# Half-head tiles for RoPE, and values stored as rows of tokens, in a two-layer transformer kernel

## The chip, the cores and the metric

One core of one Trainium2 chip runs the whole program. A core has TensorE (matrix products into PSUM), VectorE, ScalarE, GpSimd and SyncE, which here only issues DMAs; 16 DMA engines move data between SBUF and HBM. The metric is device microseconds of one execution. Profiles come from one further execution.

## The reference

Input x is (2, 1024, 512) in float32. Four blocks follow, each added to x: attention A, a feed-forward block with LoRA, attention B, the same feed-forward block again. The change touches attention A, and of B only how values are stored. Attention A, with 32 heads of 16:

```python
q = (xn @ Wq).reshape(B, S, H, Dh)          # xn: layer norm of x
kv_latent = xn @ Wc                          # 64 wide
k = (kv_latent @ Wk).reshape(B, S, H, Dh)
v = (kv_latent @ Wv).reshape(B, S, H, Dh)
q = q * cos + rotate_half(q) * sin           # rotate_half: [-x2, x1] of a head's two halves
k = k * cos + rotate_half(k) * sin
probs = softmax(q @ k.T / sqrt(Dh))          # no mask
x = x + (probs @ v) @ Wo
```

Attention B has a causal mask, ALiBi and biases, and no RoPE.

## The kernel before, in words

The program runs in stages, with a meeting of all engines between two: `project_a` (projections of A), the run of attention A, `output_and_ffn` (which also projects B's queries, keys and values), the run of attention B, and a last `output_and_ffn`. Within a stage each engine has its own written order of work, and semaphores alone tie the engines.

`project_a` works on NC = 4 chunks of 512 tokens, two for each of the two sequences. TensorE's order in chunk c: the latent; query tile 0; the four key tiles (128 dimensions = 8 heads, by 512 tokens); the four value tiles (128 tokens by 512); the rotated key tiles; the turns (transposes) of the next chunk's normalised input; query tiles 1, 2, two rotated tiles, query tile 3, two rotated tiles. A rotated tile is a product of a constant +1/-1 matrix `rot` with the plain tile (L1050 to L1057). The tasks take the 8 PSUM banks in turn (`bank_plan`), in the last chunk five banks, since three then belong to the early maxima of the first attention's scores.

The path of one tile i (0 to 3 keys, 4 to 7 queries), number n = 8c + i: ScalarE copies the product to SBUF (`copy_plain`, L1111); GpSimd multiplies by the cosines (L1190, three buffers, so it runs at most three tiles ahead); VectorE multiplies the rotated tile, out of PSUM, by the sines (L1220) and adds (L1224), giving `roped`; ScalarE rounds it to the high part (`high`, L1124), VectorE takes the low part (`low`, L1229), one tile behind; SyncE stores both parts. There are four buffers of parts: `high` waits until the store of four tiles ago has landed.

Values: ScalarE copies a tile out of PSUM into one of two buffers (L1156); from the third tile on it waits for the landing of the store of two tiles ago.

ScalarE's order in a chunk: key copies 0 to 3; value tiles 0 to 3; high 0, 1, turned input; high 2, turned input, query copy 1; high 3, query copies 2, 3; high 4, 5; the next chunk's latent and query copy 0; high 6, 7. VectorE's: tiles 0 to 3 with the low parts behind them, the low parts of the turned input, tiles 4 and 5, the normalisation of chunk c + 2 (for c = 0 and 1), tiles 6, 7. In the last chunk VectorE also takes maxima of early score pieces (L358).

SyncE's order in chunk c: the four value stores of chunk c, then the stores of the 8 tiles. So the value stores of chunk c + 1 are issued after the last query store of chunk c. In chunk 2 it also issues the first loads for the attention, between the tile stores.

Stores of attention A and B alike: `store_parts` (L778 to L788) stores a key tile with one issue (both parts, 128 rows), a query tile with two issues (64 rows and both parts each, one for each group of 4 heads). The order of rows in HBM is head by head, 16 dimensions a head. A value tile goes with one issue (L999, L1494) in 8 pieces of 512 bytes per token, one per group, so that a group's load (`load_v`, L109) reads 4 KB rows.

After the meeting the run of attention A begins: SyncE and GpSimd wait until all stores have landed; GpSimd clears two slots (L116), issues key loads (L87) and splits the first maxima (L281); TensorE makes score pieces and turns those split maxima (L331) before the first scores (L607).

Of the kernel before, what the change touches and what calls it, by code (L numbers as in the profile page):

```python
# [55 lines left out]
class Slot:  # L56
# [735 lines left out]
def stored_counts(uses):  # L792

    return 16 * (uses + uses // 2)


class Stores:
# [3 lines left out]
    def __init__(self, nc, ctx, tag):  # L801
        self.parts = [ctx.enter_context(nc.semaphore(f"{tag}_parts_stored{i}")) for i in range(PARTS)]
        self.v = [ctx.enter_context(nc.semaphore(f"{tag}_v_stored{i}")) for i in range(2)]

    def wait(self, e, batches):
        for i in range(PARTS):
            e.wait_ge(self.parts[i], stored_counts(batches * 2 * 2 * KC // PARTS))
# [78 lines left out]
def project_a(nc, env, first, early):  # L886
# [6 lines left out]
    for c in range(NC):  # L893
# [18 lines left out]
    with ExitStack() as ctx:  # L912
# [11 lines left out]
        rot = sb("rot", [P, P])  # L924
# [28 lines left out]
        cos_ready = sem("cos_ready")  # L953
        roped_ready = sem("roped_ready")
# [7 lines left out]
        def _(sp):  # L962
            for name in ("ident", "minus_half"):
                sp.dma_start(consts[name][:, :], env["ins"][name]).then_inc(consts_loaded, 16)
            for c in range(NC):
# [3 lines left out]
                if c == 0:  # L969
# [12 lines left out]
                    for t, name in ((cos, "cos"), (sin, "sin"), (rot, "rot")):  # L982
# [9 lines left out]
            for c in range(NC):  # L992
                b, half = c // 2, c % 2

                def store_v():
                    for t in range(TPC):
# [3 lines left out]
                            env["va_d"].rearrange("(g p) (k c) -> p g k c", p=P, k=8)[  # L1000
                                :, b * GPB:(b + 1) * GPB, half * TPC + t, :],
                            vt[:, n % 2, :, :].rearrange("p (g h) c -> p g (h c)", h=GH)).then_inc(v_stored[n % 2], 16)
                store_v()
                for i in range(PT):
                    n = c * PT + i
                    sp.wait_ge(low_ready, n + 1)
                    store_parts(sp, env["qa_d"], env["ka_d"], c, i, parts[:, n % PARTS, :, :],
# [19 lines left out]
        def _(pe):  # L1027
# [21 lines left out]
            pe.wait_ge(table_loaded, 48)  # L1049
            for c in range(NC):  # L1050
                def rotated(i):
                    task = ("rotated", c, i)
                    banks.wait_empty(pe, task)

                    banks.wait_drained(pe, plain_task(c, i))
                    pe.matmul(banks.out(task), rot[:, :], plain(i),
                              start=True, stop=True).then_inc(banks.fill(task), 1)  # L1057
# [26 lines left out]
                for i in range(KC):  # L1084
# [803 lines left out]
```

## Time and profile before

| what | us |
|---|---|
| median of 3 runs | 1765.24 (1760.79 to 1771.05) |
| the profiled execution | 1764.37 |
| its span | 1762.2 |
| TensorE busy | 1643.6 (93%) |
| VectorE busy | 1402.5 (80%) |
| ScalarE busy | 969.0 (55%) |
| GpSimd busy | 213.8 (12%) |
| `project_a`, to the meeting | about 184 |

Times in rows are microseconds from the span's start unless they are called ns. PE is TensorE, PEld its weight loads, DVE VectorE, ACT ScalarE, POOL GpSimd, SPq SyncE's issues. L12 is line 12 of the kernel; a tensor is named by the memory that it lies in, so `w_q` is `roped` and the product with the sines, `w_o` the value buffers, `o_memory` and `w_proj` the plain tiles and the product with the cosines. In brackets stands the idle time before an instruction and what ended it.

### The profile page before, as it was taken

How to read it: one execution, taken by the hardware profiler on the slowest of the kernel's cores; microseconds unless marked ns; L12 is line 12 of the kernel's file. 1: busy time of each engine (PE TensorE's matmuls, PEld its weight loads, DVE VectorE, ACT ScalarE, POOL GpSimd, SP SyncE). 2: the span in 40 equal slices, each digit the busy share in tenths (PEclk: the TensorE clock that was granted, in tenths of full speed). 3: DMA queues.
4: the chain of work that ended last, by engine and by line, in shares of the span. 5: the costliest groups of instructions: out<-in, count | busy, mean ns of one | idle time of the engine just before them, and what ended most of it. 6: DMA issues, size and time to landing. Idle time of an engine off the chain costs nothing. (4 is left out here: it accounts for less than half of the span.)

```text
span 1762.2 us, 32974 instructions
## 1 busy us (share of the span) xinstructions
PE 1643.6 (93%) x13040; PEld 848.8 (48%) x13040; DVE 1402.5 (80%) x2959; ACT 969.0 (55%) x1095; POOL 213.8 (12%) x272
## 2 busy tenths in 40 slices
PE   6898999999999999999999999999999999999888
PEld 3554333333333333333344777655545555554667
DVE  3776799999999999999548364568898888899675
ACT  2433277777777777777821112126666666667210
POOL 3332200000000000000013021020101000003331
PEclk9999699999999999999999999989999999999999
DMA  7766433333333333331140433773645454542211
GB/s 212 224 169 197 91 57 61 75 62 61 61 60 62 62 61 65 61 59 59 57 157 24 143 102 112 213 158 58 112 82 92 77 93 78 95 77 87 88 69 72
DMA packets 116801, 167.58 MB, mean 95 GB/s; under 512 B 20772, under 2 KB 58036, under 8 KB 116532
## 3 DMA queue, kind: packets, MB, share of 16 engines
q1 hardware_dynamic: 115176, 160.99, 39.8%
q0 software_dynamic: 1472, 4.49, 1.3%
q8 instruction: 103, 1.69, 0.4%
q14 instruction: 50, 0.41, 0.1%
HBM read 100.41 MB, written 64.50 MB: 94 GB/s over the span
## 5 line engine op out<-in xcount | busy, mean ns | idle before, releaser
L358 DVE TENSOR_REDUCE mxp<-ps_m 128x1 f32<-128x512 f32 x1280 | 798.7, 684 | 69.5 <-PE ps_m L324 64.2
L686 ACT ACTIVATE a_p<-a_ps_s 128x1024 f32<-128x1024 f32 x512 | 522.6, 1025 | 149.1 <-PE a_ps_s L607 132.4
L686 ACT ACTIVATE b_p<-b_ps_s 128x1024 f32<-128x1024 f32 (+1 forms) x320 | 294.9, 939 | 158.5 <-PE b_ps_s L607 155.2
L355 DVE CUSTOM_DVE_ANT_0 ps_m<-ps_m,b_masks 128x128 f32<-128x128 f32 (+3 forms) x512 | 240.0, 517 | 43.6 <-PE ps_m L324 39.5
L324 PE MATMUL ps_m<-slot_qk 62*128 62x512 f32 (+3 forms) x624 | 230.9, 451 | 12.2 <-DVE mxp L358 8.9
L324 PE MATMUL ps_m<-a_slot_qk 62*128 62x512 f32 x640 | 237.6, 449 | 0.8
L607 PE MATMUL a_ps_s<-a_slot_qk 64*128 64x512 f32 x640 | 231.6, 442 | 1.7 <-DMA a_slot_qk<-cturned 0.5
L631 PE MATMUL a_ps_o<-a_p,a_slot_v 128*32 128x256 f32 x2560 | 205.6, 390 | 9.9 <-ACT a_p L686 5.4
L607 PEld LDWEIGHTS a_ps_s<-a_slot_qk 64*128 64x128 f32 x640 | 96.2, 185 | 129.4 <-issue 122.7
L281 POOL CAST cparts<-negm 128x16 fp32r<-128x16 f32 x64 | 12.6, 197 | 1119.3 <-DVE negm L364 1119.3
L607 PE MATMUL a_ps_s<-slot_qk 64*128 64x512 f32 x384 | 136.4, 455 | 0.7
L631 PE MATMUL a_ps_o<-a_p,slot_memory 128*32 128x256 f32 x1536 | 124.1, 393 | 7.3 <-ACT a_p L686 3.3
L324 PEld LDWEIGHTS ps_m<-slot_qk 62*128 62x128 f32 x624 | 101.3, 190 | 39.8 <-DVE mxp L358 27.7
L631 PEld LDWEIGHTS a_ps_o<-a_p,a_slot_v 128*32 128x32 f32 x2560 | 54.8, 108 | 114.2 <-ACT a_p L686 100.5
L587 PE MATMUL b_ps_s<-b_masks 64*128 64x64 bf16 x1024 | 102.1, 197 | 3.0 <-PEq L1402 2.6
L324 PEld LDWEIGHTS ps_m<-a_slot_qk 62*128 62x128 f32 x640 | 99.2, 184 | 9.2 <-DVE mxp L358 7.9
L324 PE MATMUL ps_m<-o_qk 62*128 62x512 f32 (+3 forms) x288 | 94.7, 408 | 6.9 <-issue 2.7
L607 PEld LDWEIGHTS a_ps_s<-slot_qk 64*128 64x128 f32 x384 | 56.4, 188 | 78.6 <-issue 74.8
L324 PE MATMUL ps_m<-second_qk 62*128 62x512 f32 (+2 forms) x240 | 87.2, 415 | 3.2 <-DVE mxp L358 1.9
L607 PE MATMUL b_ps_s<-o_qk 64*128 64x512 f32 (+3 forms) x288 | 85.4, 426 | 0.0
L587 PEld LDWEIGHTS b_ps_s<-b_masks 64*128 64x128 bf16 x1024 | 54.8, 96 | 59.1 <-issue 45.1
L1594 ACT ACTIVATE slot_memory<-mid_ps,b_qk 128x512 fp32r<-128x512 f32 x23 | 15.8, 689 | 103.3 <-PE mid_ps L822 94.0
(217 smaller groups left out, 2420.5 us busy)
## 6 DMA issues: line engine op xcount, KB each, us to landing
va_groups<-w_o SPq DMA_DIRECT2D x16, 512.0 KB, 3.6
ka_parts<-pa_parts SPq DMA_DIRECT2D x16, 512.0 KB, 3.9
qa_parts<-pa_parts SPq DMA_DIRECT2D x32, 256.0 KB, 3.7
kb_parts<-slot_memory SPq DMA_DIRECT2D x16, 512.0 KB, 3.9
qb_parts<-slot_memory SPq DMA_DIRECT2D x32, 256.0 KB, 3.4
vb_groups<-w_proj SPq DMA_DIRECT2D x16, 512.0 KB, 3.4
a_slot_qk<-qa_parts SPq DMA_DIRECT2D x60, 128.0 KB, 4.3
a_slot_qk<-ka_parts SPq DMA_DIRECT2D x48, 128.0 KB, 6.6
```

What stands on the lines that cost most here:

```text
L281: pool.tensor_copy(cparts[:, :, 0, :], split(negm[:, :])).then_inc(high_ready, 1)
L324: pe.matmul(ps_m[:, bank_of(g, i), 0:keys], q, k, start=True, stop=True).then_inc(piece_ready, 1)
L355: dve.tensor_tensor_reduce(from_, from_, mask_of_query[:, CHUNK - keys:], 1.0, LOWEST, ALU.add, ALU.max, accum_out=to).then_inc(piece_take ...
L358: dve.tensor_reduce(to, from_, AX.X, ALU.max).then_inc(piece_taken, 1)
L587: pe.matmul(to[:, half * ROW_TILE:(half + 1) * ROW_TILE], mask[tile, half, :], half_ident[tile, :], start=(half == 0), stop=False, skip_gr ...
L607: mm = pe.matmul(to[:, at:at + n], k, q, start=not diagonal, stop=True, skip_group_check=diagonal)
L631: mm = pe.matmul(ps_o[VW * h:VW * (h + 1), off:off + n], slots[j].v[:, kt, VW * h:VW * (h + 1)], p_sb[:, (2 * u + h // 2) % NP, h % 2, at: ...
L686: act.activation(p_sb[:, (2 * u + pair) % NP, :, off:CHUNK], ps_s[:, 2 * pair:2 * pair + 2, off:CHUNK], ACT.Exp, scale=scale).then_inc(exp ...
L1594: act.activation(parts[:, n % PARTS, 0, :], banks.out(("qk", c, i)), ACT.Identity, bias=bias_of(i)).then_inc(high_ready, 1)
```

## The change

The columns of Wq and Wk are reordered on the host: the 512 dimensions form two groups of 16 heads, and each group is two tiles of 128, one with the first 8 dimensions of its 16 heads, one with the second 8. A tile's partner in the rotation is then the tile i ^ 1 at the same rows. The rotated products, their matrix and its load go; VectorE multiplies the partner's plain copy (now from SBUF) by the sines, and adds or subtracts. The tables of cosines and sines have 8 frequencies repeated 16 times. The parts still lie in HBM head by head, so the stores of attention A gather them: two issues for a key tile (one for each part) and eight for a query tile (four groups of 4 heads, two parts). Attention B's tiles are stored as before. In both attentions the values lie in HBM as rows of tokens: a value tile's store writes 4 KB pieces, and a group's load reads pieces of 512 bytes.

```diff
+def store_halves(sp, q_d, k_d, c, i, parts, sem):
+    b, half = c // 2, c % 2
+    m, a = divmod(i % KC, 2)
+    if i < KC:
+        row = b * D + m * 2 * P
+        for w in range(2):
+            heads = k_d[w, row:row + 2 * P, half * CHUNK:(half + 1) * CHUNK].rearrange("(h a d) t -> a h d t", a=2, d=DH // 2)
+            sp.dma_start(heads[a], parts[:, w, :].bitcast(F32)).then_inc(sem, 16)
+    else:
+        n = 2 * P // GD
+        for g in range(n):
+            row = ((b * GPB + m * n + g) * 2 + half) * GD
+            rows = slice(g * (P // n), (g + 1) * (P // n))
+            for w in range(2):
+                heads = q_d[w, row:row + GD, :].rearrange("(h a d) t -> a h d t", a=2, d=DH // 2)
+                sp.dma_start(heads[a], parts[rows, w, :].bitcast(F32)).then_inc(sem, 16)
...
 @@ project_a, the order of tasks (it also sets the banks) @@
         order += [("v", c, t) for t in range(TPC)]
-        order += [("rotated", c, m) for m in range(KC)]
         order += turn_tasks[c + 1] if c + 1 < NC else []
-        order += [("q", c, 1), ("q", c, 2), ("rotated", c, KC), ("rotated", c, KC + 1), ("q", c, 3),
-                  ("rotated", c, KC + 2), ("rotated", c, KC + 3)]
+        order += [("q", c, m) for m in range(1, KC)]
...
 @@ project_a, TensorE @@
-                for i in range(KC):
-                    rotated(i)
...
                 query(1, lambda half: maxima(0, half))
                 query(2, lambda half: maxima(1 + half, 2 + half))
                 maxima(3, 4)
-                rotated(KC)
-                rotated(KC + 1)
                 query(3, lambda half: maxima(4 + half, 5 + half))
-                maxima(6, 7)
-                rotated(KC + 2)
-                rotated(KC + 3)
-                maxima(7, early.pieces // PAIR)
+                maxima(6, early.pieces // PAIR)
...
 @@ project_a, ScalarE, copy_plain @@
-                    act.wait_ge(roped_ready, (c - 1) * PT + i + 1)
+                    act.wait_ge(roped_ready, (c - 1) * PT + (i | 1) + 1)
...
 @@ project_a, VectorE, rope @@
-                banks.wait_full(dve, task)
+                banks.wait_drained(dve, plain_task(c, i ^ 1))
...
-                dve.tensor_tensor(by_sin[:, :], banks.out(task), sin[:, at:at + CHUNK],
-                                  ALU.mult).then_inc(banks.drain(task), 1)
-                banks.wait_drained(dve, task)
+                dve.tensor_tensor(by_sin[:, :], plain(i ^ 1), sin[:, at:at + CHUNK], ALU.mult).then_inc(sin_ready, 1)
+                dve.wait_ge(sin_ready, n + 1)
                 dve.wait_ge(cos_ready, n + 1)
                 dve.tensor_tensor(roped[:, n % MIX, :], by_cos[:, n % MIX, :], by_sin[:, :],
-                                  ALU.add).then_inc(roped_ready, 1)
+                                  ALU.add if i % 2 else ALU.subtract).then_inc(roped_ready, 1)
...
 @@ SyncE, value stores (attention B alike), and Slot.load_v @@
                         sp.dma_start(
-                            env["va_d"].rearrange("(g p) (k c) -> p g k c", p=P, k=8)[
-                                :, b * GPB:(b + 1) * GPB, half * TPC + t, :],
-                            vt[:, n % 2, :, :].rearrange("p (g h) c -> p g (h c)", h=GH)).then_inc(v_stored[n % 2], 16)
+                            env["va_d"][b * P:(b + 1) * P, bass.ds((half * TPC + t) * H * VW, H * VW)],
+                            vt[:, n % 2, :, :].rearrange("p h c -> p (h c)")).then_inc(v_stored[n % 2], 16)
...
-        e.dma_start(self.v[:, :, :], v_d[bass.ds(g * P, P), :].rearrange("p (k c) -> p k c", k=8)
-                    ).then_inc(loaded, 16)
+        b, own = divmod(g, GPB)
+        groups = v_d[b * P:(b + 1) * P, :].rearrange("p (k g c) -> p g k c", k=8, g=GPB)
+        e.dma_start(self.v[:, :, :], groups[:, own, :, :]).then_inc(loaded, 16)
```

## Rows read from the trace of the kernel before

**Rows 1.** The page, part 1: busy us (share of the span) x instructions.
```profile
PE 1643.6 (93%) x13040; PEld 848.8 (48%) x13040; DVE 1402.5 (80%) x2959; ACT 969.0 (55%) x1095; POOL 213.8 (12%) x272
```

**Rows 2.** Windows, one chunk of the stage: busy us, then granted clock, DMA share, GB/s.
```profile
78.00:115.00 37.00, 32.90 (x108) 19.71 (x108) 25.85 (x41) 13.54 (x25) 10.95 (x9) 0.91 0.55 166
```

**Rows 3.** Timeline (start, us, then the work) of TensorE: rotations, turns.
```profile
72.21 1.12 PE L1056 MATMUL pa_ps<-w_proj,pa_rot 128*128 128x512 f32 x2
...
75.75 1.04 PE L881 MATMUL pa_ps<-ident,ffn_memory 128*128 128x128 f32 x8
...
80.69 1.11 PE L881 MATMUL pa_ps<-ident,ffn_memory 128*128 128x128 f32 x4 [3.91 <-ACT w_o L1156]
```

**Rows 4.** Timeline of ScalarE: value tile 2 and what follows it.
```profile
80.04 0.60 ACT L1156 ACTIVATE w_o<-pa_ps 128x512 f32<-128x512 f32 x1 [6.28 <-DMA va_groups<-w_o]
...
82.04 1.14 ACT L1124 ACTIVATE pa_parts<-w_q 128x512 fp32r<-128x512 f32 x2
```

**Rows 5.** Timeline of VectorE: first and last low parts, last maxima.
```profile
46.08 0.68 DVE L1229 TENSOR_TENSOR pa_parts<-w_q,pa_parts 128x512 fp32r<-128x512 f32 x1
...
68.10 0.68 DVE L1229 TENSOR_TENSOR pa_parts<-w_q,pa_parts 128x512 fp32r<-128x512 f32 x1
...
82.70 0.69 DVE L1229 TENSOR_TENSOR pa_parts<-w_q,pa_parts 128x512 fp32r<-128x512 f32 x1 [5.06 <-ACT pa_parts L1124]
...
105.68 0.68 DVE L1229 TENSOR_TENSOR pa_parts<-w_q,pa_parts 128x512 fp32r<-128x512 f32 x1
...
119.44 0.69 DVE L1229 TENSOR_TENSOR pa_parts<-w_q,pa_parts 128x512 fp32r<-128x512 f32 x1 [4.22 <-ACT pa_parts L1124]
...
133.04 1.42 DVE L1229 TENSOR_TENSOR pa_parts<-w_q,pa_parts 128x512 fp32r<-128x512 f32 x1 [1.15 <-ACT pa_parts L1124]
...
152.14 0.69 DVE L1229 TENSOR_TENSOR pa_parts<-w_q,pa_parts 128x512 fp32r<-128x512 f32 x1 [1.42 <-ACT pa_parts L1124]
...
179.13 4.87 DVE L358 TENSOR_REDUCE mxp<-ps_m 128x1 f32<-128x512 f32 x8
```

**Rows 6.** Timeline of SyncE's queue: query stores, value stores.
```profile
59.07 15.15 SPq L788 DMA_DIRECT2D qa_parts<-pa_parts  x8
74.27 8.26 SPq L999 DMA_DIRECT2D va_groups<-w_o  x4
...
173.59 7.14 SPq L788 DMA_DIRECT2D qa_parts<-pa_parts  x8
```

**Rows 7.** Groups by line to 215 us: busy us, mean ns, idle before.
```profile
L1224 DVE TENSOR_TENSOR w_q<-o_memory,w_q 128x512 f32<-128x512 f32 x32 | 26.3, 821 | 1.1
...
L1190 POOL TENSOR_TENSOR o_memory<-w_proj,pa_cos 128x512 f32<-128x512 f32 x16 | 20.0, 1270 | 31.1 <-ACT w_proj L1111 22.2 <-DVE w_q L1224 8.9
...
L1056 PE MATMUL pa_ps<-o_memory,pa_rot 128*128 128x512 f32 x22 | 11.2, 611 | 0.0
```

**Rows 8.** By line: ns of one issue on SyncE (min/median/max).
```profile
L783 SPq DMA_DIRECT2D ka_parts<-pa_parts x16: 359/360/1483, 46.8 to 166.9; - x16
...
L788 SPq DMA_DIRECT2D qa_parts<-pa_parts x32: 574/608/1213, 59.1 to 179.9; - x32
...
L536 SPq DMA_DIRECT2D oa_sums<-second_v x128: 407/422/1857, 231.1 to 886.0; - x128
...
L533 SPq DMA_DIRECT2D za_sums<-second_v x32: 536/550/557, 230.5 to 884.0; - x32
```

**Rows 9.** Windows, while only loads of reciprocals (L1342, 8 heads) land.
```profile
1663.60:1664.80 1.20, 1.20 (x7) 0.99 (x6) 1.16 (x3) 0.00 (x0) 0.54 (x2) 1.00 0.53 203
```

**Rows 10.** DMA issues: KB of each, median us from issue to landing.
```profile
va_groups<-w_o SPq DMA_DIRECT2D x16, 512.0 KB, 3.6
...
out<-x_sb SPq DMA_DIRECT2D x16, 256.0 KB, 2.1
```

**Rows 11.** Timeline of GpSimd behind the meeting at the stage's end.
```profile
184.53 6.96 POOL L116 MEMSET a_slot_qk<- 128x4096 f32 x2 [11.51 <-POOLq L912]
...
194.62 0.21 POOL L281 CAST cparts<-negm 128x16 fp32r<-128x16 f32 x1
```

More of the change, by code:

```diff
@@ L953, in project_a @@
         cos_ready = sem("cos_ready")
+        sin_ready = sem("sin_ready")
         roped_ready = sem("roped_ready")
@@ L981, in _ @@
                     sp.dma_start(w["v"][:, :], env["Wv"]).then_inc(attn_loaded, 16)
-                    for t, name in ((cos, "cos"), (sin, "sin"), (rot, "rot")):
+                    for t, name in ((cos, "cos"), (sin, "sin")):
                         sp.dma_start(t[:, :], env[name]).then_inc(table_loaded, 16)
@@ L1006, in _ @@
                     sp.wait_ge(low_ready, n + 1)
-                    store_parts(sp, env["qa_d"], env["ka_d"], c, i, parts[:, n % PARTS, :, :],
+                    store_halves(sp, env["qa_d"], env["ka_d"], c, i, parts[:, n % PARTS, :, :],
                                 parts_stored[n % PARTS])
@@ L1048, in _ @@
             pe.wait_ge(w_split, 2)
-            pe.wait_ge(table_loaded, 48)
             for c in range(NC):
[L1051 to L1057, printed above, removed]
                 x_parts = [lambda kc: xnt[:, c % 2, kc, :], lambda kc: xnt_low[:, c % 2, kc, :]]
@@ L1121, in high @@
                 if n >= PARTS:
-                    act.wait_ge(parts_stored[n % PARTS], stored_counts(n // PARTS))
+                    act.wait_ge(parts_stored[n % PARTS], early.stores.counts(n // PARTS))
                 act.wait_ge(roped_ready, n + 1)
@@ L1591, in high @@
                 if n >= PARTS:
-                    act.wait_ge(parts_stored[n % PARTS], stored_counts(n // PARTS))
+                    act.wait_ge(parts_stored[n % PARTS], early.stores.counts(n // PARTS))
                 banks.wait_full(act, ("qk", c, i))
@@ L1800, in build @@
                 sb("cparts", [P, PAIR, SHIFT_ROWS, 4 * GH // PAIR], F32R), sb("cturned", [SHIFT_ROWS * 4 * GH, P]))
-        early_a = Early(nc, ctx, "a", False, consts, [first], ps_m, rows, Stores(nc, ctx, "a"), 24)
-        early_b = Early(nc, ctx, "b", True, consts, [first_b, second_b], ps_m, rows, Stores(nc, ctx, "b"), 48)
+        early_a = Early(nc, ctx, "a", False, consts, [first], ps_m, rows, Stores(nc, ctx, "a", 2, 2 * (2 * P // GD)), 24)
+        early_b = Early(nc, ctx, "b", True, consts, [first_b, second_b], ps_m, rows, Stores(nc, ctx, "b", 1, P // GD), 48)
         with ExitStack() as weights:
@@ L1838, in shape_constants @@
     freqs = np.arange(S, dtype=np.float32)[:, None] * inv_freq
-    angle = np.concatenate([freqs, freqs], axis=-1).T
-    rot = np.zeros((P, P), np.float32)
-    for i in range(P):
-        if i % DH < DH // 2:
-            rot[i + DH // 2, i] = -1.0
-        else:
-            rot[i - DH // 2, i] = 1.0
+    angle = freqs.T
     row, column = (np.arange(P) % ROW_TILE)[:, None], np.arange(P)[None, :]
@@ L1865, in shape_constants, with halves_apart @@
     }
+def halves_apart(w):
+    return np.ascontiguousarray(w.reshape(-1, H // 16, 16, 2, DH // 2).transpose(0, 1, 3, 2, 4).reshape(w.shape))
 NAMES = ["L0_attn_a_hidden_states", "L0_attn_a_Wq", "L0_attn_a_Wc", "L0_attn_a_Wk", "L0_attn_a_Wv",
@@ L1878 @@
     host = {name: np.ascontiguousarray(inputs[name]) for name in NAMES}
+    for name in ("L0_attn_a_Wq", "L0_attn_a_Wk"):
+        host[name] = halves_apart(host[name])
     host.update(shape_constants())
```

31 lines of the change are left out of this document (14 added, 17 removed).

## The prediction

> **What bounds the kernel now.** I read the page's busy shares first: TensorE is busy 1643.6 of 1762.2 us, VectorE 1402.5 [rows 1]. For the whole span that says "TensorE", but the RoPE work stands only in the first stage, the projections before the first attention (about 0 to 184 us), so I read that stage alone. In the stretch from 78 to 115 us TensorE is busy 32.9 of 37 us, VectorE 25.9, ScalarE 13.5, at a granted clock of 0.91 [rows 2]. Nearly full, but not full: the TensorE rows show a hole of 3.91 us in the turns of the next chunk, ended by ScalarE's copy of a value tile [rows 3], and that copy itself had waited 6.28 us for a DMA, the store of the value tile whose buffer it needs [rows 4].
>
> So I followed the ring that repeats once per chunk of 512 tokens. Call T the moment at which VectorE starts the first low part (L1229) of a chunk: 46.08, 82.70, 119.44, 152.14 us [rows 5]. The ring: the low parts of the last three query tiles are made; SyncE issues their stores; only then, by its program, the value stores of the next chunk; ScalarE can copy value tile 2 once value tile 0 has landed, then tile 3, then the first high part; VectorE's first low part waits for that. From the start of that copy of tile 2 to T it is 82.70 - 80.04 = 2.66 us [rows 4, 5]. SyncE is full there: 8 query issues in 15.15 us paced by the tiles, then the first value store at 74.27, seen by ScalarE at 80.04 [rows 4, 6]. The ring has periods of 36.6, 36.7 and 32.7 us [rows 5]. The reader is to see that TensorE is nearly full, yet the ring through SyncE also closes in the same time: taking TensorE work away does not shorten it.
>
> **Part by part.**
>
> *Rotation products, removed.* 32 products, 64 instructions in four groups (22, 16, 16, 10) [rows 7]. Their pitch: 8 instructions from 72.21 to the next work at 75.75, 0.44 us each [rows 3]; 64 x 0.44 = 28 us of TensorE time. That is the most this edit can give, if TensorE sets the pace. By the ring it gives VectorE only the waits for a rotated tile and for a late query tile: about 3 us of each middle period. The turns of the next chunk get other PSUM banks (the key tiles' instead of the value tiles'), so TensorE's 3.9 us hole goes as well; what is late next is the same ScalarE chain, since VectorE's low part still waits for it.
>
> *VectorE's product with the sine, from PSUM to SBUF.* One operation for one. But VectorE's sum, which reads two SBUF tiles, has a mean of 821 ns [rows 7] where the low part, of the same size, mostly takes 690 [rows 5]; I read the difference as time in which it stands until GpSimd's product, 1.3 us each [rows 7], is over. The sine product now reads two SBUF tiles as well: 0 to 1.3 us per tile (nothing, or a whole GpSimd product as behind that mean); most GpSimd products fall into time in which VectorE waits anyway, so I take 1 us per chunk. The Trainium skill, "SBUF — State Buffer", section "Who interferes with whom", states it as an exclusive lock that a VectorE operation with two SBUF inputs and a GpSimd operation that reads SBUF hold for their whole length. By that rule all 8 sine products of a chunk could be held, half a GpSimd product each, 8 x 0.65 = 5 us more per chunk; the trace's sums, in the same position, lose 0.13 us on average.
>
> *Query stores, 2 issues per tile become 8.* Each is 32 rows of 2 KB (64 KB) and goes to 4 heads. SyncE's cost of one: 0.36 us for 128 rows, 0.61 for the present 64-row query store, 0.42 for 16 rows, 0.55 for 4 rows [rows 8]; with the gap of 0.05 between issues I take 0.60 (nearest: the same tensor, and the 4-row store) and keep 0.46 and 0.66 as ends. 16 query tiles x 6 more issues x 0.6 = 58 us of SyncE time. *Their transfer.* When only the loads of reciprocals run, whose source is 8 heads, the DMA share stands at 0.53 with 203 GB/s [rows 9]: half the engines work. The new store's destination has 4 heads as its outer dimension, so I take a quarter: 102 GB/s, 64 KB in 0.65 us, a tile in 5.2 us where the present tile needs some 1.3 at full width. Bounds: 0.16 us (all engines) to 0.97 (0.65 stretched by 1.5, as the value store at 74.27 that was seen after 5.8 us against a median of 3.6 [rows 4, 6, 10]). The Trainium skill, "DMA: Bandwidth & Descriptors", section "Why a DMA increments its semaphore by 16 and not by 1", gives the rule: the number of engines is the largest up to 16 that divides the slowest dimension of both sides, here 4. By the rule the transfer is my 0.65 us; by the row alone, half the engines, it would be 0.33 and SyncE's 0.60 would bind. The same page, section "Issuing engines are not separate DMA queues", calls the sequencer's time "usually small relative to the DMA itself"; by that the 58 us would cost nothing. The rows above say otherwise: 0.6 against 0.65.
>
> *Key stores, 1 issue becomes 2* of 128 rows: 4 x 0.4 us per chunk, in a stretch where SyncE has room: nothing.
>
> *Value stores in 4 KB pieces.* 512 KB lands in 3.6 us now, 256 KB of 2 KB rows in 2.1 [rows 10]; twice the bytes at full width (2 x 203 GB/s) is 0.65 more: 2.8 us. 0.8 us per landing is gained; bounds 0 and 1.5. *Value loads in 512-byte pieces* (both attentions): the store of that shape takes 3.6 us, they are issued a step ahead: nothing. The second layer's value stores: nothing to -1 us, I take 0.
>
> **The sum along the ring.** After n query stores of 8 issues each, the first value tile has landed n x 8 x 0.65 + 2.8 us after the burst began, then 2.65 us to T. (By SyncE alone it is 0.60 instead of 0.65.)
> - Chunk 0 to 1: T comes 1.2 us earlier in chunk 0 (faster value landings); the low part of query tile 1 ended at 68.78 [rows 5]; less 1.2, less 1.6 of waits gone, plus 1 of lock: 67.0. Burst of three tiles: 67.0 + 15.6 + 2.8 + 2.65 = 88.1 against 82.70: +5.4.
> - Chunk 1 to 2: the burst begins at T + 23.7 (106.4 - 82.7) [rows 5]; less 3, plus 1: T + 21.5. Period 21.5 + 21.05 = 42.6 against 36.7: +5.9.
> - Chunk 2 to 3: no normalisation lies between the query tiles, so all four are one burst from T + 15 (the row at 133.04 ends at 134.46 [rows 5]), less 3: T + 12. Period 12 + 20.8 + 5.45 = 38.2 against 32.7: +5.5.
> - End of the stage. Now all engines meet at 184.5, T + 32.4, when VectorE's maxima are over [rows 5, 11]; the query stores began at 173.59, T + 21.4 [rows 6]. Then: T + 20 and 32 issues of 0.60, SyncE arrives at T + 39.4: +7.0.
> - GpSimd behind it: it waits until the stores have landed, clears two buffers, loads keys and splits the maxima at 194.62, 10 us after the meeting [rows 11], and TensorE waits for that. The last store lands at T + 20 + 20.8 + 2.1 = T + 42.9, 3.5 after the new meeting: +3.5.
>
> Together +27.3 on the profiled execution's 1764.4 us (1762.2 span and 2.2 around it): 1791.7; that execution is 0.9 below the median, so I say 1792.
>
> **Rivals.**
> 1. *The pieces spread over all engines* (or half): SyncE's 0.60 binds alone. Three bursts gain 1.2, 1.2 and 1.6, the last landing falls to the meeting's time: 27.3 - 4 - 3 = +20, 1784. For it: no row here shows 4 heads. Against: the row at half share.
> 2. *Four engines, and crowded* (0.97 us): +13, +13.5, +15.8 at the periods, +7.0, +13.7 behind GpSimd: up to 1827, more likely halfway, 1810. For it: the value store's 5.8 us; against: loads stay within their 203 GB/s.
> 3. *Short issues* (0.46 us) and spread pieces: 24 x 0.46 + 5.45 = 16.5 after the burst: +0.7, +1.3, -0.5, +2.8 and 2 for GpSimd: +6, 1770: no difference to tell.
> 4. *The other side: the ring does not hold VectorE.* If a query store costs SyncE under 0.22 us (24 in the present 5.4 us between the low part and the first value store) and lands as fast, the value copies come when VectorE still works, and VectorE's own 26 us per chunk is the bound: -9, -9, -5 at the periods and -3 at the end: 1738. It decides at T: this needs T to follow the last low part within 4 us instead of 11. For it: 28 us of TensorE work really go; against: every issue row of [rows 8] is above 0.35.
>
> **How the numbers follow.** Forecast 0.45, rival 1 0.20, rival 2 0.12, rival 3 0.12, rival 4 0.11. A difference of 0.5% (8.8 us) is what a measurement can tell. Slower: 0.45 + 0.20 + 0.12 = 0.77; within: 0.12; faster: 0.11. The range 1769 to 1814 takes in rivals 1 and 3 and the likelier half of 2, and leaves out 4.
>
> **What would show it.** In the changed kernel: no rotation rows; query stores 128 of 64 KB with about 0.6 us each; SyncE busy without a gap from the query stores to the value stores; ScalarE's wait for the value store near 10 us, not 6; periods of T of 43 and 38 us; the DMA share near 0.25 in the bursts; TensorE idle for some 15 us per chunk, its clock below 0.91; the meeting near 211 us instead of 184. Wrong: periods below 37 us (rivals 3, 4), a share above 0.5 in the bursts (rival 1), or any difference after the first attention has begun.

## The result, and the profile after

The changed kernel takes 1803.25 us (median of 4 runs, 1800.37 to 1811.83) where the kernel before, run beside it, takes 1763.01: a ratio of 1.0222, 95% interval 1.0192 to 1.0252. It is slower by 2.2%, some 40 us; forecast were 1792 us, a range of 1769 to 1814, and "slower" with 0.77. The profiled execution took 1800.37 us (span 1798.1), 36.0 more than that of before; the differences below are taken between these two executions.

The page, part 1 (against [rows 1]): TensorE is busy 13.6 us less and VectorE 11.1 us more in a span that is 35.9 longer.
```profile
PE 1630.0 (91%) x12976; PEld 845.1 (47%) x12976; DVE 1413.6 (79%) x2959; ACT 967.5 (54%) x1095; POOL 219.2 (12%) x272
```
Windows of the changed kernel (busy us of PE, PEld, DVE, ACT, POOL; granted clock; DMA share; GB/s). The first is the stretch of [rows 2]; the second lies in the query burst of chunk 1 (a burst is a run of query stores that SyncE issues one behind the other), the next three are the loads and the burst of chunk 2, the last is the burst of chunk 3.
```profile
78.00:115.00 37.00, 25.52 (x81) 16.55 (x80) 27.23 (x41) 13.32 (x25) 10.99 (x8) 0.82 0.46 156
106.00:121.00 15.00, 10.09 (x40) 8.49 (x40) 9.23 (x9) 3.98 (x8) 7.63 (x5) 0.77 0.24 87
130.00:142.00 12.00, 8.45 (x29) 5.54 (x28) 11.86 (x18) 5.32 (x10) 4.22 (x3) 0.80 1.00 202
142.00:150.00 8.00, 4.93 (x12) 1.79 (x11) 2.57 (x5) 2.26 (x5) 0.00 (x0) 0.90 0.93 240
150.00:163.00 13.00, 10.90 (x21) 5.16 (x21) 6.61 (x5) 2.63 (x6) 7.56 (x5) 0.67 0.26 101
205.00:220.00 15.00, 3.62 (x6) 1.42 (x5) 4.97 (x9) 0.00 (x0) 0.00 (x0) 0.50 0.26 96
```
TensorE went from 32.9 to 25.5 busy us of 37: the rotation products are gone, and yet the stage is longer. VectorE's timeline at T, the first low part of each chunk (against [rows 5]):
```profile
43.36 0.69 DVE L1235 TENSOR_TENSOR pa_parts<-w_q,pa_parts 128x512 fp32r<-128x512 f32 x1 [1.59 <-ACT pa_parts L1130]
...
85.79 0.69 DVE L1235 TENSOR_TENSOR pa_parts<-w_q,pa_parts 128x512 fp32r<-128x512 f32 x1 [12.40 <-ACT pa_parts L1130]
...
128.41 0.69 DVE L1235 TENSOR_TENSOR pa_parts<-w_q,pa_parts 128x512 fp32r<-128x512 f32 x1 [12.54 <-ACT pa_parts L1130]
...
174.51 0.69 DVE L1235 TENSOR_TENSOR pa_parts<-w_q,pa_parts 128x512 fp32r<-128x512 f32 x1 [17.44 <-ACT pa_parts L1130]
```
The periods are 42.4, 42.6 and 46.1 us (before 36.6, 36.7, 32.7), and VectorE now stands idle for 12 to 17 us ahead of T in chunks 1 to 3. The releaser named is ScalarE's high part; that stood behind ScalarE's copy of value tile 2, which waited for the store of tile 0 (against [rows 4]):
```profile
83.41 0.60 ACT L1162 ACTIVATE w_o<-pa_ps 128x512 f32<-128x512 f32 x1 [14.56 <-DMA va_tokens<-w_o]
```
and SyncE's queue shows why that store was late (against [rows 6]; start, us, line, count): from chunk 1 on, the value stores begin 0.04 us after the query burst of the chunk before has ended.
```profile
55.12 23.74 SPq L811 DMA_DIRECT2D qa_parts<-pa_parts  x32
78.90 6.68 SPq L1019 DMA_DIRECT2D va_tokens<-w_o  x4
...
96.62 24.67 SPq L811 DMA_DIRECT2D qa_parts<-pa_parts  x32
121.33 6.87 SPq L1019 DMA_DIRECT2D va_tokens<-w_o  x4
...
142.43 21.00 SPq L811 DMA_DIRECT2D qa_parts<-pa_parts  x32
163.47 10.83 SPq L1019 DMA_DIRECT2D va_tokens<-w_o  x4
175.22 17.21 SPq L803 DMA_DIRECT2D ka_parts<-pa_parts  x8
199.56 20.42 SPq L811 DMA_DIRECT2D qa_parts<-pa_parts  x32
```
The cost of the issues, and their landings (against [rows 8] and [rows 10]; ns min/median/max; the last line is of the value stores):
```profile
L811 SPq DMA_DIRECT2D qa_parts<-pa_parts x128: 582/582/1237, 55.1 to 219.4; - x128
...
L803 SPq DMA_DIRECT2D ka_parts<-pa_parts x32: 517/599/1828, 44.1 to 191.8; - x32
...
DMA to landing us min/median/max: 2.6/3.1/9.4
```
The end of the stage, on GpSimd (against [rows 11], whose clearing begins at 184.53):
```profile
223.54 6.96 POOL L118 MEMSET a_slot_qk<- 128x4096 f32 x2 [24.56 <-DMA qa_parts<-pa_parts]
...
233.63 0.21 POOL L283 CAST cparts<-negm 128x16 fp32r<-128x16 f32 x1
```

| step | forecast | measured |
|---|---|---|
| T of chunk 1 | +5.4 | +3.1 (85.79 against 82.70) |
| period 1 to 2 | +5.9 | +5.9 (42.6 against 36.7) |
| period 2 to 3 | +5.5 | +13.4 (46.1 against 32.7) |
| from T of chunk 3 to GpSimd's clearing | +7.0 + 3.5 | +16.6 (49.0 against 32.4) |
| all that follows | 0 | -3.1 (1574.6 against 1577.7) |
| sum | +27.3 | +35.9 |

Of the signs that the forecast named, the issues, the unbroken queue, the first two periods and the DMA share came as said. ScalarE's wait for the value store came longer, 14.6, 14.7 and 19.2 us for the 10 said, and SyncE's last issue ended at 219.98 us, where the meeting was said to be near 211.

### The profile page after: what moved, and what is told of

Read it like the earlier page. It is cut to its first block and busy times, and to the rows that moved or that the text cites. A ratio compares the mean times of both kernels' runs of the same rounds, so it can differ in the third digit from the quotient of the medians.

```text
span 1798.1 us, 32925 instructions
## 1 busy us (share of the span) xinstructions
PE 1630.0 (91%) x12976; PEld 845.1 (47%) x12976; DVE 1413.6 (79%) x2959; ACT 967.5 (54%) x1095; POOL 219.2 (12%) x272
## 5 line engine op out<-in xcount | busy, mean ns | idle before, releaser
L283 POOL CAST cparts<-negm 128x16 fp32r<-128x16 f32 x64 | 12.6, 197 | 1118.1 <-DVE negm L366 1118.1
L633 PE MATMUL b_ps_o<-b_p,v_memory 128*32 128x256 f32 (+2 forms) x864 | 68.7, 401 | 4.0 <-ACT b_p L688 2.6
```

The source lines that it names most:

```text
L283: pool.tensor_copy(cparts[:, :, 0, :], split(negm[:, :])).then_inc(high_ready, 1)
L633: mm = pe.matmul(ps_o[VW * h:VW * (h + 1), off:off + n], slots[j].v[:, kt, VW * h:VW * (h + 1)], p_sb[:, (2 * u + h // 2) % NP, h % 2, at: ...
```

## The experiments

Where two kernels differ by under 0.5%, the stage's own times in their traces are read beside the whole time.

**Is it the issues, and is it the four engines?** e1_wide gives the queries the keys' layout, so that a pair of query tiles leaves in 4 stores of 128 rows over all engines, not in 16 of 32 rows over four; e2_cut keeps all engines, but cuts each of these stores into four column slices, and so has as many issues as the changed kernel, in pieces of 512 bytes. Both kernels also load the queries with two DMAs where one stood, and store attention B's query tiles with one issue each. (In the cuts of code here the ends of some lines are left out.)
```diff
-        n = 2 * P // GD
-        for g in range(n):
-            row = ((b * GPB + m * n + g) * 2 + half) * GD
-            rows = slice(g * (P // n), (g + 1) * (P // n))
-            for w in range(2):
-                heads = q_d[w, row:row + GD, :].rearrange("(h a d) t -> a h d t", ...)
-                sp.dma_start(heads[a], parts[rows, w, :].bitcast(F32))
+    for w in range(2):
+        heads = to[w, row:row + 2 * P, half * CHUNK:(half + 1) * CHUNK].rearrange("(h a d) t -> a h d t", ...)
+        sp.dma_start(heads[a], parts[:, w, :].bitcast(F32))
# e2_cut: four slices t of 128 columns in place of the whole half
```


> The changed kernel with the queries in the keys' layout in HBM (rows of 1024 tokens), so that a query tile goes with two issues of 128 rows, whose outer dimension is 16 heads; a group's query load is split into two DMAs each. Theory (the ring is held by SyncE's issues and by transfers on 4 of 16 engines): SyncE's burst of query stores is over within 5 us, the value tile lands 3 us later, and the periods of T fall from 42.4, 42.6, 46.1 us to about 31, 31, 27, the meeting from 220.8 us to about 165: some 1748 us, 15 below the kernel before. Rival (VectorE's sine product out of SBUF, held by GpSimd's lock, is the cost): the periods stay above 37 us, and the time within 10 us of 1803.

Measured: 1760.62 us, ratio 0.9972 (0.9953 to 0.9992).

> As e1_wide, but a query tile again goes with 8 issues of 64 KB, each now 128 rows by 128 columns (pieces of 512 bytes) whose outer dimension is 16 heads: the number of issues of the changed kernel on all 16 engines. Theory with the issues as the binding part: 24 issues of 0.4 to 0.6 us still stand ahead of the value stores, but the value tile lands 3 us after its issue even in chunk 3: periods near 40, 40, 39, the time 1785 to 1795 us. Rival (the 4 engines alone bind): as e1_wide, 1750 us.

Measured: 1799.48 us, ratio 1.0197 (1.0169 to 1.0225). SyncE's queue between chunks 0 and 1, first of e1_wide, then of e2_cut:
```profile
55.09 14.10 SPq L798 DMA_DIRECT2D qa_parts<-pa_parts  x8
69.28 8.67 SPq L1006 DMA_DIRECT2D va_tokens<-w_o  x4
```
```profile
54.85 25.64 SPq L802 DMA_DIRECT2D qa_parts<-pa_parts  x32
80.54 5.17 SPq L1010 DMA_DIRECT2D va_tokens<-w_o  x4
```
With few issues the periods of T are 33.9, 32.4 and 31.3, and the loss of the change is gone (my 1748 was 13 too low: other things, below, hold the stage there; the burst was paced by the tiles and took 14.10 us, not 5, and the value store was seen after 5.0 us, 69.28 to 74.24, not 3). With many issues and all engines they are 41.9, 41.2 and 43.1: within 1.5 us of the changed kernel at the first two, 3 below it at the third. So 39 of the 43 us between e1_wide and the changed kernel come back with the number of issues. The small pieces are not the cause: from 107 to 121 us, where e2_cut's SyncE issues without a pause, the DMA share is 0.41 and the rate 98 GB/s, so the DMA engines are far from full. The 3.8 us between e2_cut and the changed kernel lie within the intervals and can't be given to the four engines by the whole time. In the stage e2_cut's clearing comes 6.0 us earlier (217.50 against 223.54). In the chunk with the slot's loads ScalarE sees the value store after 2.93 us there (164.89 to 167.82), and after 8.65 us in the changed kernel (163.47 to 172.12):
```profile
167.82 0.60 ACT L1153 ACTIVATE w_o<-pa_ps 128x512 f32<-128x512 f32 x1 [15.98 <-DMA va_tokens<-w_o]
```

**The layout of the values**, by itself: e3_after_groups is the changed kernel with the values grouped by heads as before, e4_before_tokens the kernel before with the values as rows of tokens.
```diff
-  env["va_d"][b * P:(b + 1) * P, bass.ds((half * TPC + t) * H * VW, H * VW)]
+  env["va_d"].rearrange("(g p) (k c) -> p g k c", p=P, k=8)[:, b * GPB:(b + 1) * GPB, half * TPC + t, :]
# e4_before_tokens: the other way round, in the kernel before
```


> The changed kernel with the old layout of the values in both attentions (stores in pieces of 512 bytes, loads in rows of 4 KB). Theory: the value store lands 0.5 us later each time and nothing else moves: 2 to 4 us above the changed kernel. Rival (the first group's value load in 512-byte pieces is what fills the queues before the last burst): the period of T from chunk 2 to 3 falls by 3 us or more, and the time is 2 us below the changed kernel or better.

Measured: 1806.18 us, ratio 1.0244 (1.0207 to 1.0280); periods 43.1, 43.0, 45.2. That is 2.9 us above the changed kernel, as expected, though within the intervals. The third period fell by 0.9 us where the rival asked for 3: the first group's value load in small pieces is not the main part of what fills the queues there.

> The kernel before with the new layout of the values alone. Theory: the ring gains 0.5 to 1 us per period and 1 to 2 us at the end of the second projection: 2 to 5 us faster than the kernel before. Rival: the loads in 512-byte pieces cost more than that, and it is slower.

Measured: 1763.16 us, ratio 0.9990 (0.9968 to 1.0013). The token rows bring T forward by 1.7 us in chunk 0 (44.42 against 46.08) and GpSimd's clearing by 4.9 (179.68 against 184.53); in the whole time no difference can be told either way.

**The order of issues, the loads, the values' buffers.** e5_after_act is the changed kernel with the value stores issued by ScalarE behind its own copies, e6_wide_act the same in e1_wide, e7_after_late the changed kernel with the first slot's loads in chunk 3.
```diff
+                    banks.wait_drained(act, task)     # e5, e6: behind the copy of a value tile
+                    act.dma_start(env["va_d"][...], vt[:, n % 2, :, :]...).then_inc(v_stored[n % 2], 16)
-                    if c == 2:                        # e7
-                        for share in (2 * i, 2 * i + 1):
+                    if c == 3:
+                        for share in range(4 * i, 4 * i + 4):
```


> The changed kernel, with one move: the value stores of the first stage are issued by ScalarE right behind its copy of the value tile, no longer by SyncE behind the query stores of the chunk before. All 128 query issues of 32 rows stay as they are. If it is the order of issues in SyncE that holds VectorE (my theory), the periods of T fall from 42.4, 42.6, 46.1 us to about 34, 34, 36 (SyncE has 25 to 28 us of issues per chunk left, less than VectorE and TensorE need), the meeting of the engines comes near 195 instead of 221 us, and the time is about 1772. The end of the stage stays slow in this theory, since 32 issues of 0.63 us still stand behind the last chunk's query tiles. If it is the four DMA engines that hold it, the value stores, which need all sixteen, land as late as before (8 to 10 us) and the periods stay above 40: 1798. If it is VectorE's new product against GpSimd, or TensorE at half its clock, nothing moves: 1803.

Measured: 1791.87 us, ratio 1.0156 (1.0139 to 1.0173). T comes at 45.30, 78.90, 115.19 and 156.55, periods of 33.6, 36.3 and 41.4. The first is the one I expected: the value stores' place behind the burst made 8.8 us of that period. The others are not (34 and 36 expected for the second and third, and 1772 us in all, 20 too low), and ScalarE's timeline says why: its high parts of the key tiles wait for the four buffers of parts, the first two of these for query stores that SyncE has only just issued.
```profile
121.14 0.63 ACT L1122 ACTIVATE pa_parts<-w_q 128x512 fp32r<-128x512 f32 x1 [4.49 <-DMA qa_parts<-pa_parts]
...
126.33 0.63 ACT L1122 ACTIVATE pa_parts<-w_q 128x512 fp32r<-128x512 f32 x1 [3.10 <-DMA qa_parts<-pa_parts]
...
134.53 0.63 ACT L1122 ACTIVATE pa_parts<-w_q 128x512 fp32r<-128x512 f32 x1 [6.09 <-DMA ka_parts<-pa_parts]
```
There are two rings through SyncE, then, by the values' buffers and by the parts' buffers; with the first one opened the second still holds the periods at 36.3 and 41.4. The order of the issues alone is a quarter of the loss (11 of 40 us).

> The kernel with queries in the keys' layout (two 128-row stores per pair of query tiles), with the value stores issued by ScalarE as well. There VectorE's first low part still waited 3.9, 2.3 and 2.9 us behind the value copies. Ring theory: these waits go, the periods fall from 33.9, 32.4, 31.3 to about 31, 31, 30, and the time from 1760.6 to about 1755. Rival: TensorE (now at a clock of 0.8 and below) or ScalarE, which now issues 16 stores itself, sets the pace: 1760 or a little above.

Measured: 1761.15 us, ratio 0.9987 (0.9972 to 1.0002): no gain, against my theory. ScalarE copies value tile 0, issues its store, and waits for its landing all the same:
```profile
69.64 0.33 ACTq L1145 DMA_DIRECT2D va_tokens<-w_o  x1
...
75.28 0.60 ACT L1141 ACTIVATE w_o<-pa_ps 128x512 f32<-128x512 f32 x1 [4.30 <-DMA va_tokens<-w_o]
```
Whoever issues, two buffers for four value tiles cost a landing ahead of the first high part.

> The changed kernel with the loads of the first attention's slot issued in chunk 3 (four shares behind the first key store and four behind the second), not in chunk 2. Theory: the period from chunk 2 to 3 was 46.1 us where the sum gave 38.2 because these loads fill the DMA queues and SyncE just ahead of and in that burst; without them it falls to 39 to 41, and the loads cost up to 3 us at the start of chunk 3 instead: in all 4 us less, 1799. Rival: the excess is SyncE's price of the issues (0.656 us in that burst, key stores of 0.6) and TensorE's half clock, so the period stays at 45 and the time at 1803.

Measured: 1816.23 us, ratio 1.0291 (1.0274 to 1.0307). T of chunks 2 and 3 in its VectorE timeline:
```profile
129.43 0.69 DVE L1235 TENSOR_TENSOR pa_parts<-w_q,pa_parts 128x512 fp32r<-128x512 f32 x1 [12.31 <-ACT pa_parts L1130]
...
168.74 0.69 DVE L1235 TENSOR_TENSOR pa_parts<-w_q,pa_parts 128x512 fp32r<-128x512 f32 x1 [15.75 <-ACT pa_parts L1130]
```
The period is 39.3 us, as expected, so 6.8 of the 7.9 us that my sum missed there came from the loads. ScalarE sees the value store after 4.84 us (161.50 to 166.34):
```profile
166.34 0.60 ACT L1162 ACTIVATE w_o<-pa_ps 128x512 f32<-128x512 f32 x1 [16.54 <-DMA va_tokens<-w_o]
```
The whole time was not as expected, 1799: I had priced the late loads at 3 us, and the last query burst began at T + 43.4 (212.18) where in the changed kernel it began at T + 25.0. The maxima of chunk 3 read that slot, and they stand ahead of the query tiles in TensorE's program; TensorE stood for 38.95 us until a load of the slot had landed.

**What is the removal itself worth?** e8_before_wide is the kernel before with one store per query tile and the values as rows of tokens; against it, e1_wide has half-head tiles: no rotation products, VectorE's sine product out of SBUF, and two stores per tile where e8_before_wide has one. The pair prices these together. e9_wide_order and e10_before_order add one change of order to e1_wide and e8_before_wide, e11_after_order to the changed kernel: ScalarE makes the first two high parts before it copies value tiles 2 and 3.
```diff
+                value(0)
+                value(1)
                 high(c, 0)
                 for i in range(1, KC):
                     high(c, i)
+                    if i == 1:
+                        value(2)
+                        value(3)
```


> The kernel before, with the rotation products, but with the queries in the keys' layout (one store of 128 rows per query tile) and the values as rows of tokens: against the kernel e1_wide it differs only in the removal of the rotation products (half-head tiles), so the pair prices that removal by itself. With the ring eased on both sides, I expect periods of 36, 35 and 31 here against 33.9, 32.4 and 31.3 there: 1763, and so 3 us for the removal. If TensorE's 28 us of rotation products were what sets the pace once the ring is eased, this kernel would be 15 us or more slower than e1_wide: 1775.

Measured: 1760.90 us, ratio 0.9983 (0.9967 to 1.0000): equal to e1_wide. Periods 34.4, 35.2 and 30.2; GpSimd's clearing comes 3.6 us later than there (179.54 against 175.99), which the whole time doesn't show. I had expected 3 us for the removal; the rival, 15 us or more, is out.

> The kernel e1_wide (queries in the keys' layout) with another order in ScalarE's program: it copies value tiles 0 and 1, makes the high parts of key tiles 0 and 1, and only then copies value tiles 2 and 3. In e6_wide_act VectorE still waited 3.5, 2.6 and 3.0 us, since ScalarE's copy of value tile 2 waited 4.3 us for the buffer of tile 0, whoever issued the store. Theory: two buffers for four value tiles, copied ahead of the first high part, are what holds the first low part once SyncE's issues are few; with this order the waits of about 3 us go at all four chunks, the periods fall to about 30, 30 and 29, and the time to about 1751. Rival: TensorE, whose granted clock is 0.8 and below here, or VectorE's own 28 us per chunk sets the pace, and the waits only move to a later tile: 1759.

Measured: 1755.88 us, ratio 0.9940 (0.9924 to 0.9956). T at 43.59, 74.64, 107.04, 138.09 (periods 31.1, 32.4, 31.1), GpSimd's clearing at 171.84. That lies between the 1751 that I expected and the rival's 1759: 4.7 us below e1_wide, with intervals that overlap a little, and 4.2 us in the stage.

> The kernel e8_before_wide (with the rotation products) with the same order in ScalarE's program as e9_wide_order. With both rings open, the pair prices the removal of the rotation products where nothing else should stand in for them. TensorE was busy 31.0 of 32 us in the stretch 78 to 110 there, so I expect little from the order: periods of 33.5, 34 and 30, time 1758, some 7 us above e9_wide_order. Rival: the removal is worth nothing here either, because VectorE's sine products against GpSimd cost what the rotation waits did: both kernels within 2 us.

Measured: 1761.19 us, ratio 0.9975 (0.9963 to 0.9987). GpSimd's clearing at 178.86. With few issues and the new order the removal, its extra stores included, is worth 5.3 us (7.0 in the stage; 7 expected). The order of ScalarE gains nothing where the rotations stand (e8 to e10: 1760.90 to 1761.19). VectorE's waits in e10_before_order from 42 to 140 us (us in total, times, longest) show what is held there: the sine products wait for rotated tiles, 19.9 us in six waits.
```profile
DVE w_q L1219 <- PE ps_m L1051: 10.4, 4, 3.8
DVE w_q L1219 <- PE pa_ps L1051: 9.5, 2, 7.6
```


> The changed kernel with the same order in ScalarE's program. SyncE's bursts of 24 and 32 issues stay. Ring theory: from the landing of value tile 0 to the next burst the path loses the first two key tiles (2 x 1.93 us), which VectorE now does ahead of it: periods of 38.5, 38.7 and 42 us against 42.4, 42.6 and 46.1, 12 us less in all, 1791. Rival: SyncE's issues as such bound the stage (32 query issues, 8 key issues and 4 value stores come to 29 us, with the landings behind them), or the four buffers of parts, which open again only when a query tile's eight pieces have landed, hold the key tiles at the same place: 1800 or more.

Measured: 1792.33 us, ratio 1.0152 (1.0131 to 1.0174), GpSimd's clearing at 210.96, 12.6 earlier than in the changed kernel where 12 were expected. The time is the expected one, but the parts of the sum are not: I had expected 3.9 us from each of three periods. The first value store of chunk 2 is issued 3.0 us earlier than in the changed kernel (118.29 against 121.33), that of chunk 3 only 3.6 us earlier (159.88 against 163.47), and the other 9.0 us come in the last chunk. In chunk 2, from 125.17 us on, SyncE has its key stores, the slot's fifteen loads and the burst to issue and waits for VectorE 0.3 us in all; there the rival (SyncE's issues as such bound the stage) holds. That the total met the forecast is partly luck.

**The two engines on SBUF.** e12_keys_cos is e9_wide_order with the cosine products of the key tiles made by VectorE, not by GpSimd.
```diff
+                if i < KC:
+                    dve.tensor_tensor(by_cos[:, n % MIX, :], plain(i), cos[:, at:at + CHUNK], ALU.mult)
```


> The kernel e9_wide_order with the cosine products of the four key tiles of each chunk made by VectorE, ahead of its sum, and no longer by GpSimd (which keeps those of the query tiles). In e9_wide_order VectorE is busy 29.8 of 33 us, and at each chunk's start five of its RoPE operations on SBUF tiles take 1.45, 1.64, 1.59, 1.66 and 1.76 us where the same operations take 0.69 later in the chunk, while GpSimd's four products of the key tiles run. If the two engines hold each other up there (theory: two SBUF inputs on VectorE against GpSimd), the five go back to 0.69: 8.1 - 3.5 = 4.6 us gained, less 4 x 0.69 = 2.8 for the products VectorE now makes: 1.9 us less per chunk, periods of about 29, 30.5 and 29 against 31.1, 32.4 and 31.1, and about 1749. Rival: the long operations only contain a wait for GpSimd's product or for ScalarE's copy of the plain tile, and no interference: VectorE then gains at most the waits of the two sums (2 us) and pays 2.8: 1757 to 1762.

Measured: 1749.40 us (6 runs, 1747.14 to 1750.66), ratio 0.9906 (0.9883 to 0.9930), the fastest of all and faster than both kernels. VectorE at the same place, start of chunk 1: first in e9_wide_order, then in e12_keys_cos.
```profile
68.26 1.44 DVE L1218 TENSOR_TENSOR w_q<-w_proj,pa_sin 128x512 f32<-128x512 f32 x1 [0.28 <-ACT w_proj L1102]
69.73 1.64 DVE L1221 TENSOR_TENSOR w_q<-o_memory,w_q 128x512 f32<-128x512 f32 x1
...
74.64 0.68 DVE L1226 TENSOR_TENSOR pa_parts<-w_q,pa_parts 128x512 fp32r<-128x512 f32 x1
```
```profile
66.23 0.69 DVE L1219 TENSOR_TENSOR w_q<-w_proj,pa_sin 128x512 f32<-128x512 f32 x1 [0.28 <-ACT w_proj L1102]
66.84 0.68 DVE L1222 TENSOR_TENSOR o_memory<-w_proj,pa_cos 128x512 f32<-128x512 f32 x1
67.56 0.69 DVE L1227 TENSOR_TENSOR w_q<-o_memory,w_q 128x512 f32<-128x512 f32 x1
...
70.29 0.68 DVE L1232 TENSOR_TENSOR pa_parts<-w_q,pa_parts 128x512 fp32r<-128x512 f32 x1
```
Two tiles take VectorE 6.4 us with GpSimd at work beside it (four products from 67.89, 6.28 us) and 4.1 alone, though it makes a third product for each. In e12_keys_cos GpSimd begins at 70.46, on a query tile, and VectorE's next sine product is long again:
```profile
70.89 1.78 DVE L1219 TENSOR_TENSOR w_q<-w_proj,pa_sin 128x512 f32<-128x512 f32 x1
```
The groups from 40 to 170 us (lines; count, busy us, mean ns), e9_wide_order and then e12_keys_cos:
```profile
L1221 DVE TENSOR_TENSOR w_q<-o_memory,w_q 128x512 f32<-128x512 f32 x32 | 29.8, 931 | 1.1
...
L1218 DVE TENSOR_TENSOR w_q<-w_proj,pa_sin 128x512 f32<-128x512 f32 x15 | 20.4, 1363 | 1.3 <-ACT w_proj L1102 0.8
```
```profile
L1227 DVE TENSOR_TENSOR w_q<-o_memory,w_q 128x512 f32<-128x512 f32 x31 | 21.5, 692 | 2.2
...
L1219 DVE TENSOR_TENSOR w_q<-w_proj,pa_sin 128x512 f32<-128x512 f32 x14 | 14.0, 999 | 1.2 <-ACT w_proj L1102 0.8
```
The long durations were interference, not a wait: the rival said 1757 to 1762, and the sine product, which uses nothing of GpSimd's, falls from 1.44 us to 0.69. The periods became 30.2, 30.2 and 30.4 (29, 30.5 and 29 expected), and GpSimd's clearing comes 5.9 us earlier than in e9_wide_order (165.92 against 171.84). 3.5 of these 5.9 us were gained ahead of the first T (40.10 against 43.59), which the expectation did not separate.

## Why the prediction was right, and where its sizes were off

- **The ring, not TensorE, sets T.** Right. TensorE lost 7.4 busy us in the chunk of [rows 2] and the chunk grew by 6. e1_wide takes away three quarters of the query issues and the whole loss goes; e2_cut gives the issues back, on all engines, and 39 us return. The period from chunk 1 to 2 was given as 42.6 and measured as 42.6, and that close agreement is luck: the burst began at T + 20.5 for T + 21.5, took 15.0 us for 15.6, and the value store was seen after 4.7 us for 2.8. (The start, 23.7 less 3 plus 1, is 21.7 and not 21.5.) What I did not see is that the ring is double: the buffers of the parts close it too (e5_after_act), so moving the value stores out of SyncE's queue alone is worth 11 us.
- **0.60 us per issue against 0.65 of transfer on a quarter of the engines.** The issue is right: 0.582 median, 0.61 to 0.66 with the gaps in bursts (20.42/32 = 0.64, 21.00/32 = 0.66). So is the quarter: the share in the bursts is 0.24 to 0.26 with 87 to 101 GB/s, where rival 1 asked for over 0.5. (By the Trainium skill, "DMA: Bandwidth & Descriptors", section "Why a DMA increments its semaphore by 16 and not by 1", a DMA uses the largest number of engines up to 16 that divides the slowest dimension of both sides, here 4; the trace agrees.) The two are too near each other for the periods to tell them apart; e2_cut did: the same issues on all engines take 1799.5 against 1803.3, so SyncE's issues are enough to bind. The Trainium skill's words on issuing, in section "Issuing engines are not separate DMA queues" of the same page ("usually small relative to the DMA itself"), do not hold here: 96 more issues for the same bytes cost 39 us.
- **T of chunk 1, +5.4 forecast, +3.1 measured.** The first chunk came 2.7 us early, not 1.2 (43.36 against 46.08), and VectorE's low part of query tile 1 ended at 63.9, not 67.0. The value store landed later than said, 4.5 us from its issue to ScalarE's copy (78.90 to 83.41) against 2.8.
- **Period from chunk 2 to 3, +5.5 forecast, +13.4 measured: the term most off.** "T + 12" for the start of the burst was T + 14.0: the key stores, which I put at nothing, cost 0.60 each and twice as many (1.16 for a pair, where one of 0.36 had stood), just where the slot's fifteen loads leave SyncE no room. The value store's landing was 8.65 us (163.47 to 172.12) where the sum had 2.8. Together 2.0 + 5.85 = 7.9, the whole miss (the burst's own 0.2 more and the last step's 0.25 less cancel). The share of 1.00 and 0.93 in 130 to 150 us shows full queues ahead of the burst, and e7_after_late, without the loads there, has a period of 39.3, with the burst at T + 11.9: without the loads the same key stores do cost nothing. The value store is late only where the loads and the stores on four engines come together: 8.65 us here, 4.84 in e7_after_late (no loads), 2.93 in e2_cut (loads, but all engines). The 2.8 us were those of a nearly empty queue; the fastest landing is 2.6.
- **End of the stage, +10.5 forecast, +16.6 measured.** "T + 20" for the last burst was T + 25.0; the 32 issues took 20.4 for 19.4, and GpSimd came 3.6 us after the last, 3.5 forecast. The kernel before has the burst at T + 21.4, so 1.4 of the 5.0 us is a gain that I had put there and that did not come; the other 3.6 are 2.5 us more of VectorE's waits for the maxima (6.4 against 3.9) and 1.1 for one low part that took 1.75. The waits are TensorE's. It had stood for 19.94 us ahead of the first maximum of chunk 3, and six products then took 2.93 us (granted clock 0.50, that is 1.2 GHz) where the same six take 1.66 from 188.90 on (1.00, 2.4 GHz). The stretch from 174.5 to 199.5 has a granted clock of 0.64; in the kernel before, 152.1 to 173.6 has 0.92.
```profile
174.50:199.50 25.00, 15.37 (x38) 8.58 (x38) 18.42 (x29) 4.46 (x8) 4.24 (x3) 0.64 0.35 110
```
  The kernel before has one such slow set of six as well (158.12 to 161.05, clock 0.50), and VectorE's first wait is nearly the same (2.67 against 2.30). Most of the difference is the third wait, 2.67 against 0.82: there the changed kernel's clock is again 0.50 (193.9 to 196.8), after 2.24 us in which TensorE waited for VectorE, and the clock of the kernel before is 1.00. I had said that the clock would fall, and had priced it at nothing. That the clock is the cause was not tried apart from the wait that lowers it.
- **The sine product against GpSimd: 1 us per chunk.** Too small as a duration and without effect here. In the changed kernel four operations of a chunk's start take 1.43, 1.64, 1.57 and 1.65 us, 3.5 us above 0.69 each; but VectorE then waits 12.4 us for the values. Where the ring is open it counts: e12_keys_cos is 6.5 us below e9_wide_order. The rule that the forecast weighed ("SBUF — State Buffer", section "Who interferes with whom", of the Trainium skill), some 5 us per chunk by this kernel's durations, was nearer than my 1 us: in e9_wide_order the sine products and sums are (931 - 690) x 32 + (1363 - 690) x 15 = 17.8 us above their length alone, 4.5 per chunk. Of this the sums of the kernel before already had (821 - 690) x 32 = 4.2 us, so the change added some 3.4 per chunk.
- **Values.** The landing has a median of 3.1 us against 3.6, forecast 2.8; the layout is worth 2.9 us in the changed kernel by e3_after_groups (within the intervals) and nothing to be told by e4_before_tokens. The loads in 512-byte pieces, called nothing, are one of the fifteen loads in chunk 2. With the values grouped (e3_after_groups) the value store is still seen after 7.2 us there for 8.65, and the period is 0.9 shorter: their share of the delay is some 1 to 2 us.
- **The other side** (1738, the ring does not hold VectorE) was wrong at 24 issues of 0.6 us, as its own condition says. The 28 us of rotation products come out as 5.3 us (e9 against e10), since VectorE then takes nearly the whole chunk: from 72 to 105 us it is busy 29.8 of 33 us in e9_wide_order and 24.4 in e10_before_order. TensorE is busy 31.4 of these 33 us in e9_wide_order, at a granted clock of 0.87, but VectorE waits for it nowhere from 42 to 140 us.

What is left open: the 3.1 us that the changed kernel makes up behind the stage, and the some 4 us that e1_wide, e9_wide_order, e10_before_order and e12_keys_cos lose there (1571.5 to 1571.8 us from GpSimd's split to the end of the span, against 1567.6 before). Both are within what two executions of one kernel differ by (the kernel before ranges from 1759.39 to 1771.05 beside the changed kernel). That four kernels agree to 0.3 us there speaks for a cause all the same, but e8_before_wide, with the same layouts as e10_before_order, has 1566.0; no run tells more.

## What to carry to other kernels

Count the DMA issues of a layout before its bytes. A change that frees the busiest engine but multiplies the issues of a queue that stands in a ring (part buffers, store, landing, copy) makes the ring the bound; find the queue in which two kinds of stores stand in program order and price the second behind the first. When a ring opens, look for the next one at once: here SyncE's issues, then two buffers for four value tiles, then VectorE and GpSimd at work on SBUF tiles at the same time, each worth 5 to 40 us. What one is worth depends on the others: ScalarE's new order gained 11 us in the changed kernel, 5 in e1_wide and nothing in e8_before_wide.

## What the runs showed that I had not expected

- An issue hardly gets cheaper with fewer rows: 0.582 us for 32 rows of 2 KB, 0.60 for 128 rows of half heads, and 0.36 for 128 rows with both parts in one store [rows 8]. The number of stores counts more than their size.
- Stores on four engines can delay one that needs all sixteen, if these four are behind already: in chunk 2, with the slot's loads ahead of the burst, the value store took 8.65 us until ScalarE's copy. Twelve of its sixteen landings had come after 3.5 us; the other four needed 7.1 to 8.6. Without the loads (e7_after_late) all sixteen had come after 4.8 us.
- GpSimd's cosine product takes 1.57 us (four in 6.28) beside VectorE's and 1.27 alone, and VectorE's sine product 1.44 to 1.78 and 0.69 alone: both engines lose.
